# Second graph layer: the edge pass reads its source rows through a table of tiles in memory, and two loads become one

## The chip, the cores and the metric

One Trainium2 chip (trn2), one core. The metric is the device time of one execution in microseconds. The kernel before took 4205.64 us, the median of three runs (4204.25 to 4207.73).

## What is computed

3125 nodes with 64 features and 100000 edges sorted by their destination. Two attention layers (8 heads, then 4), a layer norm, then neighbour sums with three dense layers and a second norm. One attention layer, cut to what matters:

```
xl = (x @ Wl).reshape(N, heads, Dh);  xr = (x @ Wr).reshape(N, heads, Dh)
e = leaky_relu(xl[src] + xr[dst], 0.2)
logits = einsum('ehd,hd->eh', e, att)
a = exp(logits - segment_max(logits, dst)[dst])
alpha = a / segment_sum(a, dst)[dst]
out = segment_sum(alpha[:, :, None] * xl[src], dst)      # then the mean over heads, + bias
```

## The kernel before, in words

The sorted edges are cut into 800 tiles of 125 edges (T = 125, G = 800), the nodes into 98 windows of 32 (WN, NW). A unit is a pair of a tile and a window in which the tile has edges. Units are numbered so that unit = tile + window: 897 of them, padded to 900. A tile that spans two windows is in two units, and each of its units handles only the edges of its own window. The edge pass (`edge_pass`, lines 749 to 1236) goes through 45 chunks of 20 units (CU = 20).

Each unit needs two inputs in on-chip memory. `xs` holds the 125 source rows (64 floats each, 256 bytes). GpSimd (POOL) gathers them with one indirect DMA for a unit (line 820 in the pass, line 530 ahead of it); six chunks of buffers rotate (XR = 6), so POOL waits at line 817 until the sums of chunk c - 6 are done. `xw` holds the rows of the unit's window, split into three bf16 parts, 96 rows of 128 bytes. SyncE (SP) reads the window's number into a register (line 542, with a check of its bounds) and issues one DMA from `x3_d` at that address (line 543); three buffers rotate.

TensorE (PE) turns the 20 units of a chunk in five groups of four (`turn`, lines 873 to 889). Ahead of the first group it waits for all 20 gathers and all 20 window loads. Then come the projection (line 897), the logits (906, 909), the scans for the maxima on VectorE (DVE), the weights, and some three chunks later the weighted sums (948). SP also issues, in program order for every chunk: the list of window numbers of the next chunk (536), the destination numbers `dlb` (858), four loads of `lim` and four of `pre` for the chunk before (839, 841), and a store of maxima (865). PE's order is written out by hand; SP may be up to two chunks ahead of it (line 850).

In the second layer the node rows are computed just before. Two blocks precede the edge pass: `prepare_layer` (POOL gathers the first 35 units, EARLY) and `count_tables` (POOL gathers 45 more, up to 80 = `ahead` * 20). All engines meet at the end of each block. SP loads the windows of chunk 0 in `prepare_layer` (line 617) and those of chunk 1 only once the edge pass has begun. After the last chunk POOL gathers node maxima (826). `neighbour_sums` begins with a block that splits the rows in three parts (1604 to 1616).

Of the kernel before, what the change touches and what calls it, by code (L numbers as in the profile page):

```python
# [8 lines left out]
I32 = mybir.dt.int32  # L9
# [52 lines left out]
AHEAD = (1, 4)  # L62
EARLY = 35
# [10 lines left out]
class Layer:  # L74


    def __init__(self, nm, H, Wl, Wr, att, bias, x_node, x_rows, next_table, next_node, v_d, max_d, norm):
        self.nm, self.H, self.Wl, self.Wr, self.att, self.bias = nm, H, Wl, Wr, att, bias
        self.x_node, self.x_rows, self.next_table, self.next_node = x_node, x_rows, next_table, next_node
        self.v_d, self.max_d, self.norm, self.ahead = v_d, max_d, norm, AHEAD[1 if norm else 0]  # L80
# [125 lines left out]
def build_staircase(nc, k, a, ctx0, x0):  # L206
# [4 lines left out]
    k.src_idx = sbuf(nc, ctx0, "src_idx", [T, UT], I32)  # L211
    k.win_idx = sbuf(nc, ctx0, "win_idx", [BLK, NB], I32)
# [6 lines left out]
    with ExitStack() as ctx:  # L219
# [50 lines left out]
        no_key = sbuf(nc, ctx, "no_key", [1, 1])  # L270
        ps = [psum(nc, ctx, f"ps_setup{i}") for i in range(4)]
        s = {n: k.setup.enter_context(nc.semaphore("st_" + n)) for n in (
            "load", "iota", "ident0", "ident", "dve", "dve2", "dve3", "store", "transposed", "pad",
            "load2", "sides", "last", "upto2", "node", "keys", "lim", "x_pad", "dloc", "dl0", "row0", "pre", "pre_dma", "below0", "below")}
# [5 lines left out]
        with nc.Block() as block:  # L280
            @block.sync
            def _(sp):
                sp.dma_start(dg[:], a["dst"].rearrange("(p k e) -> p k e", k=KT, e=T)).then_inc(s["load"], 16)
                ld = Dma(sp, s["load2"])
# [17 lines left out]
                xs.wait()  # L302

# [78 lines left out]
        with nc.Block() as block:  # L382
            @block.vector
            def _(dve):
# [37 lines left out]
                link(dve.tensor_copy(k.dst_local[:, 5 * BLK:UT], ps[3][0:T, 0:4 * BLK]))  # L422
                dve.wait_ge(s["keys"], 16 * (2 * NB + 1))
# [37 lines left out]
            def _(act):  # L461
                for t in range(NT):
# [8 lines left out]
            def _(pe):  # L471
                pe.wait_ge(s["dve3"], NB + 2)
                for b in range(NB):
# [4 lines left out]
                                 k.ident[0:BLK, 0:BLK]).then_inc(s["transposed"], 1)  # L478

# [67 lines left out]
def prepare_layer(nc, k, ctx, lay):  # L547
# [24 lines left out]
    lay.node_of = sbuf(nc, ctx, lay.nm + "node_of", [128, HV * 128])  # L572
    with ExitStack() as tmp:
# [27 lines left out]
        with nc.Block() as block:  # L601
            @block.sync
            def _(sp):
# [12 lines left out]
                sp.wait_ge(lay.ld_w[0], 16)  # L616
                load_windows(k, sp, lay, fixed(0))
# [3 lines left out]
            def _(pool):  # L621
# [10 lines left out]
                fetch_rows(k, pool, lay, 0, EARLY if lay.norm else lay.ahead * CU)  # L632
# [116 lines left out]
def edge_pass(nc, k, lay):  # L749
# [12 lines left out]
    with ExitStack() as ctx:  # L762
# [5 lines left out]
        lim = [sbuf(nc, ctx, f"{nm}lim{r}", [128, SL + 1]) for r in range(3)]  # L768
        pre = [sbuf(nc, ctx, f"{nm}pre{r}", [128, SL]) for r in range(3)]
# [42 lines left out]
        with nc.Block() as block:  # L812
            @block.gpsimd
            def _(pool):
                for c in map(fixed, range(lay.ahead, NCH)):
# [14 lines left out]
            def _(sp):  # L830
                sp.wait_ge(s["init"], 8)

                def limits(c):
# [38 lines left out]
            def _(pe):  # L872
# [81 lines left out]
                pe.wait_ge(s["init"], 8)  # L954
# [25 lines left out]
            def _(act):  # L980
# [52 lines left out]
                act.wait_ge(s["init"], 8)  # L1033
# [29 lines left out]
            def _(dve):  # L1063
# [31 lines left out]
                def forward(c):  # L1095

                    r = c.slot(3)
                    dve.wait_ge(ld_l[r], c.uses(3) * 128)
# [944 lines left out]
```

## Time and profile before

| | |
|---|---|
| median of 3 runs | 4205.64 us |
| the profiled execution | 4214.95 us, of which the span is 4213.1 us |
| first layer's edge pass | 188 to 1854 us |
| second layer's `prepare_layer`, `count_tables` | 1963 to 2019 us, 2022 to 2098 us |
| second layer's edge pass | 2102 to 3580 us |
| neighbour sums and dense layers | 3670 us to the end |
| busy over the span: PE, DVE, ACT, POOL, SP's share of DMA packets | 80%, 69%, 40%, 69%, 11.3% of 16 DMA engines |

Times in rows are microseconds from the start of the span, durations of single instructions in nanoseconds where a row says min/median/max. "PEclk" is the granted share of TensorE's clock. Rows of the queue engines (SPq) are issuing work: the time for which SP is occupied with an instruction, not the transfer. In brackets stands the idle time before an instruction and what ended it.

### The profile page before, as it was taken

The numbers are of one execution on the slowest core, as the hardware profiler recorded it, in microseconds if no ns is written. First come the engines' busy times: TensorE is split into PE (matmuls) and PEld (weight loads), VectorE is DVE, ScalarE is ACT, GpSimd is POOL, SyncE is SP. The second block draws the span as 40 slices with busy tenths as digits, with TensorE's granted clock in tenths as the row PEclk, the third lists the DMA queues.
The fourth block names the chain that finished last, engine by engine and source line by source line (L and its number), as shares of the span: only waits on it lengthen the run. The fifth ranks groups of instructions, "written<-read, shape, count | busy, mean of one in ns | idle before, by whom it ended". The sixth has DMA issues, their size and how long they took to land. (4 is left out here: it accounts for less than half of the span.)

```text
span 4213.1 us, 81047 instructions
## 1 busy us (share of the span) xinstructions
PE 3388.3 (80%) x24299; PEld 2227.2 (53%) x24299; DVE 2892.4 (69%) x7435; ACT 1684.6 (40%) x3682; POOL 2891.8 (69%) x2226
## 2 busy tenths in 40 slices
PE   0499999999999999965178877777877776588896
PEld 0246666666666666654135545545554554355553
DVE  3568888888888888855426655555555555499982
ACT  3354444444444444413033333333333331256651
POOL 4488888887777777163747888888888883377750
PEclk9999999999999999957579988888888887599997
DMA  2234343343333333231123333333333331112110
GB/s 57 49 61 93 86 87 87 86 86 86 84 85 84 83 84 85 56 82 50 27 50 70 76 72 69 73 67 67 72 68 67 67 67 36 40 35 44 35 41 27
DMA packets 614978, 278.31 MB, mean 66 GB/s; under 512 B 452841, under 2 KB 575117, under 8 KB 613956
## 3 DMA queue, kind: packets, MB, share of 16 engines
q1 hardware_dynamic: 266160, 103.07, 11.3%
q0 software_dynamic: 110784, 80.17, 10.8%
q10 hardware_dynamic: 237600, 89.88, 8.7%
q8 instruction: 199, 3.26, 0.3%
q14 instruction: 235, 1.93, 0.2%
HBM read 164.01 MB, written 106.40 MB: 64 GB/s over the span
## 5 line engine op out<-in xcount | busy, mean ns | idle before, releaser
L897 PE MATMUL L_e_ps_z<-L_e_xT,L_w_abs 128*128 128x500 f32 x2700 | 1504.3, 643 | 1.9 <-issue 1.5
L820 POOL DMA_INDIRECT L_e_xs<-in_x_dram,src_idx x880 | 1196.0, 1359 | 337.2 <-issue 261.3
L820 POOL DMA_INDIRECT L_e_xs<-x_d,src_idx x820 | 1077.5, 1314 | 311.3 <-issue 249.4
L948 PEld LDWEIGHTS L_e_ps_v<-L_e_xs,L_e_p 125*128 125x128 f32 x5400 | 858.7, 204 | 655.6 <-issue 589.6
L993 ACT ACTIVATE L_e_rl<-L_e_ps_z 128x500 f32<-128x500 f32 x1350 | 790.0, 587 | 818.6 <-PE L_e_ps_z L897 610.1
L948 PE MATMUL L_e_ps_v<-L_e_xs,L_e_p 125*128 125x65 f32 x5400 | 798.9, 275 | 30.1 <-DVE L_e_acc L1177 25.0
L1177 DVE SCALAR_TENSOR_TENSOR L_e_acc<-L_e_acc,L_e_row,L_e_ps_v 128x130 f32<-128x130 f32 (+1 forms) x1440 | 449.5, 312 | 416.7 <-PE L_e_ps_v L948 218.9
L884 PE MATMUL L_e_ps_x<-ident,L_e_xs 125*64 125x125 f32 x1800 | 290.7, 287 | 301.5 <-DMA L_e_xs<-x_d,src_idx 255.7
L986 ACT ACTIVATE L_e_xT<-L_e_ps_x 128x500 f32<-128x500 f32 x450 | 264.5, 588 | 606.7 <-PE L_e_ps_x L887 447.9
L897 PEld LDWEIGHTS L_e_ps_z<-L_e_xT,L_w_abs 128*128 128x128 f32 x2700 | 427.4, 198 | 80.0 <-issue 31.1
L1160 DVE TENSOR_TENSOR L_e_p<-L_e_ohc,L_e_ae 125x640 f32<-125x640 f32 x540 | 427.1, 819 | 0.0
L1650 POOL DMA_INDIRECT g_xs<-x_d,src_idx x240 | 290.7, 1211 | 163.8 <-issue 59.1
L884 PEld LDWEIGHTS L_e_ps_x<-ident,L_e_xs 125*64 125x64 f32 x1800 | 189.6, 120 | 347.1 <-DMA L_e_xs<-x_d,src_idx 265.2
L1182 DVE SCALAR_TENSOR_TENSOR L_e_acc<-L_e_acc,L_e_keep,L_e_ps_v 128x65 f32<-128x65 f32 x540 | 134.8, 277 | 315.2 <-PE L_e_ps_v L948 237.9
L1088 DVE SCALAR_TENSOR_TENSOR L_e_f<-L_e_rl,L_sign 128x500 f32<-128x500 f32 x450 | 326.3, 726 | 14.6 <-issue 9.0
L1088 DVE SCALAR_TENSOR_TENSOR L_e_f<-L_e_rl,L_sign,L_e_f 128x500 f32<-128x500 f32 x450 | 330.4, 734 | 4.4 <-ACT L_e_rl L993 0.8
L1788 DVE TENSOR_SCALAR g_ohr<-t_rows_n,t_both 125x125 bf16<-125x125 bf16 x960 | 306.8, 326 | 3.3 <-PE g_ps_c L1701 2.6
L1764 ACT ACTIVATE g_cnt<-g_ps_c 125x400 bf16<-125x400 f32 x480 | 240.0, 503 | 170.2 <-PE g_ps_c L1701 150.7
L1789 DVE TENSOR_SCALAR g_ohk<-t_keys_n,t_both 125x200 bf16<-125x200 bf16 x960 | 304.1, 318 | 0.0
L1000 ACT ACTIVATE L_e_lg<-L_e_ps_l 128x125 f32<-128x125 f32 x450 | 123.6, 275 | 335.3 <-PE L_e_ps_l L909 261.2
L1701 PE MATMUL g_ps_c<-g_ohk,g_ohr 125*125 125x200 bf16 x960 | 182.8, 274 | 62.6 <-DVE g_ohk L1789 45.3
L906 PE MATMUL L_e_ps_l<-L_e_xT,L_w_lin 128*32 128x125 f32 x3600 | 192.2, 286 | 32.3 <-DVE L_e_f L1088 32.0
(305 smaller groups left out, 3853.4 us busy)
## 6 DMA issues: line engine op xcount, KB each, us to landing
L_v_d<-L_e_acc ACTq DMA_DIRECT2D x225, 260.0 KB
L_e_dlb<-dloc_d SPq DMA_DIRECT2D x90, 468.8 KB
L_v_d<-L_e_acc ACTq DMA_DIRECT2D x225, 130.0 KB
L_e_xw<-x_d SPq DMA_DIRECT2D x1800, 12.0 KB
L_e_xs<-in_x_dram,src_idx POOLq DMA_INDIRECT x900
L_e_xs<-x_d,src_idx POOLq DMA_INDIRECT x900
g_xs<-x_d,src_idx POOLq DMA_INDIRECT x240
L_e_lim<-lim_d SPq DMA_DIRECT2D x180, 19.5 KB
```

What stands on the lines that cost most here:

```text
L820: pool.indirect_dma_start(xs[c.slot(XR)][:, n, 0:D], None, lay.x_rows, bass.IndirectOffsetOnAxis(k.src_idx[:, u:u + 1], 0)).then_inc(gath[ ...
L884: pe.transpose(ps[0:D, j * T:(j + 1) * T], xs[r][:, n, 0:D], k.ident[0:T, 0:T])
L897: pe.matmul(ps_z[(C * g + part) % ZR][:, 0:QT], lay.w_abs[:, part * 128:(part + 1) * 128], xT[q][:], start=True, stop=True).then_inc(s["z_ ...
L948: ins = pe.matmul(ps_v[u // 2 % 2][:, u % 2 * VX + v * XW:u % 2 * VX + (v + 1) * XW], p[st % 3][:, u % NQ, v, :, :].rearrange("e n h -> e ...
L986: act.activation(xT[q][:], ps_x[g % 2][:, 0:QT], ACT.Copy).then_inc(s["xT_ready"], 1)
L993: act.activation(rl[n % NE][:], ps_z[n % ZR][:, 0:QT], ACT.Relu, scale=1.0 - SLOPE).then_inc(s["relu_done"], 1)
L1088: dve.scalar_tensor_tensor(out=f[g % 3][:], in0=rl[(C * g + part) % NE][:], scalar=lay.sign[:, part:part + 1], in1=rl[(C * g) % NE][:] if ...
L1160: ins = dve.tensor_tensor(p[n % 3][:, :, v, :, :], ohc[c.slot(2)][:, us, :].unsqueeze(3).to_broadcast([T, NQ, WN, HL]), ae[c.slot(2)][:, u ...
L1177: ins = dve.scalar_tensor_tensor(out=to, in0=prev, scalar=row[c.slot(2)][:, u:u + 1], in1=ps_v[u // 2 % 2][:, u % 2 * VX:(u % 2 + 1) * VX] ...
L1650: pool.indirect_dma_start(xs[p][:, j, :], None, table, bass.IndirectOffsetOnAxis(k.src_idx[:, u:u + 1], 0)).then_inc(gath[p], 16)
L1788: dve.tensor_scalar(ohr[v % HR][:], rows_n[:], both[:, v, 0:1], None, ALU.is_equal)
L1789: dve.tensor_scalar(ohk[v % HR][:], keys_n[:], both[:, v, 1:2], None, ALU.is_equal).then_inc(s["hot"], 1)
```

## The change

It gives the second layer (`lay.norm`) another way for `xs`. POOL gathers each tile once, 800 gathers, into four buffers of ten tiles; SP stores every ten tiles into a table in memory, `tiles_d`; and for every unit SP computes tile = unit - window from the register it already has and issues one more DMA, which loads the tile's 125 rows into `xs`. The indices of the tiles (`k.src_tile`) are made once in the set-up. POOL's gathers ahead of the edge pass grow from 35 + 45 units to 50 + 50 tiles; SP stores the first eight groups of ten there. In the pass, group e + 1 is stored half a chunk before the first unit that may need it, and group e + 4 is gathered after group e is stored. In the edge pass of this layer the window loads move behind `dlb` and the limits of the chunk before. For both layers: `lim` and `pre` come with one DMA of two rows, four instead of eight in a chunk, and the run-time check of the window's bounds is gone. 15 comparisons that make `winhot8` move from `count_tables` to the first block of `neighbour_sums`. The set-up gets one load, eight transposes and two copies more.

```diff
-AHEAD = (1, 4)
-EARLY = 35
+AHEAD = (1, 5)
+EARLY = 50
+TH = CU // 2
+TR = 4
+STORED = 8
+THS = G // TH
...
+def fetch_tiles(k, pool, lay, t0, t1):
+    for t in range(t0, t1):
+        e = t // TH
+        if t % TH == 0 and e >= TR:
+            pool.wait_ge(lay.t_store[e % TR], 16 * (e // TR))
+        pool.indirect_dma_start(lay.tiles[e % TR][:, t % TH, :], None, lay.x_rows,
+                                bass.IndirectOffsetOnAxis(k.src_tile[:, t:t + 1], 0)).then_inc(lay.t_gath[e % TR], 16)
+
+def store_tiles(k, sp, lay, e):
+    sp.wait_ge(lay.t_gath[e % TR], 16 * TH * (e // TR + 1))
+    sp.dma_start(bass.AP(lay.tiles_d.tensor, e * TH * D, [[G * D, T], [1, TH * D]]),
+                 lay.tiles[e % TR][:].rearrange("p u d -> p (u d)")).then_inc(lay.t_store[e % TR], 16)
+
+def stored(sp, lay, e):
+    sp.wait_ge(lay.t_store[e % TR], 16 * (e // TR + 1))
...
 def load_windows(k, sp, lay, c):
     for n in range(CU):
-        window = sp.value_load(lay.wins[c.slot(2)][0:1, n:n + 1], min_val=0, max_val=NW - 1)
+        e = 2 * c.number + n // TH
+        if lay.norm and n % TH == 0:
+            if (c.number == 0 or e + 1 >= STORED) and e + 1 < THS:
+                store_tiles(k, sp, lay, e + 1)
+            if e < THS:
+                stored(sp, lay, e)
+        u = min(c.val(CU, n), G + NW - 2)
+        window = k.nc.values_load(lay.wins[c.slot(2)][0:1, n:n + 1], engines=[mybir.EngineType.SP], min_val=max(0, u - G + 1), max_val=min(u, NW - 1),
+                                  skip_runtime_bounds_check_because="win_idx is the least of a count's rest and NW - 1")
+        if lay.norm:
+            sp.dma_start(lay.xs[c.slot(XR)][:, n, 0:D], bass.AP(lay.tiles_d.tensor, (u - window) * D,
+                                                                [[G * D, T], [1, D]])).then_inc(lay.gath[c.slot(XR)], 16)
         sp.dma_start(lay.xw[c.slot(3)][:, n, :], bass.AP(k.x3_d.tensor, window * (WN * S3),
                                                          [[D, 3 * WN], [1, D]])).then_inc(lay.ld_x[c.slot(3)], 16)
...
@@ prepare_layer
                 sp.wait_ge(lay.ld_w[0], 16)
+                if lay.norm:
+                    store_tiles(k, sp, lay, 0)
+                    sp.wait_ge(s["ones"], XR)
                 load_windows(k, sp, lay, fixed(0))
...
-                fetch_rows(k, pool, lay, 0, EARLY if lay.norm else lay.ahead * CU)
+                if lay.norm:
+                    fetch_tiles(k, pool, lay, 0, EARLY)
+                else:
+                    fetch_rows(k, pool, lay, 0, lay.ahead * CU)
@@ edge_pass
+                if lay.norm:
+                    fetch_tiles(k, pool, lay, lay.ahead * CU, G)
+                for c in map(fixed, range(lay.ahead, 0 if lay.norm else NCH)):
...
-                        sp.dma_start(lim[r][32 * j:32 * j + H, 0:SL],
-                                     bass.AP(k.lim_d.tensor, at, [[0, H], [1, SL]])).then_inc(ld_l[r], 16)
-                        sp.dma_start(pre[r][32 * j:32 * j + H, :],
-                                     bass.AP(k.pre_d.tensor, at, [[0, H], [1, SL]])).then_inc(ld_l[r], 16)
+                        sp.dma_start(both[r][32 * j:32 * j + H, :, 0:SL],
+                                     bass.AP(k.lim_d.tensor, at, [[0, H], [SLOTS, 2], [1, SL]])).then_inc(ld_l[r], 16)
...
-                        if c.after(1):
+                        if c.after(1) and not lay.norm:
                             sp.wait_ge(ld_w[c.slot(2)], c.uses(2) * 16)
                             load_windows(k, sp, lay, c)
...
                         limits(b)
+                    if lay.norm and c.there() and c.after(1):
+                        sp.wait_ge(ld_w[c.slot(2)], c.uses(2) * 16)
+                        if c.after(XR):
+                            sp.wait_ge(s["v_ready"], c.val(CU, CU * (1 - XR)))
+                        load_windows(k, sp, lay, c)
@@ count_tables
-                fetch_rows(k, pool, lay, EARLY, lay.ahead * CU)
+                fetch_tiles(k, pool, lay, EARLY, lay.ahead * CU)
...
+                for e in range(3, STORED):
+                    store_tiles(k, sp, lay, e)
...
-                for b in range(EB):
-                    link(dve.tensor_scalar(winhot8[:, b, :, :].rearrange("u j w -> u (j w)"), wins_n[0:BU, :], unit[:, b:b + 1], None, ALU.is_equal))
@@ neighbour_sums, first block
                     dve.tensor_tensor(rest[:], x_node[:], x3[:, :, 0, :], ALU.subtract).then_inc(s["rest"], 1)
+                    for b in range(EB):
+                        dve.tensor_scalar(winhot8[:, b, :, :].rearrange("u j w -> u (j w)"), wins_n[0:BU, :], unit[:, b:b + 1], None, ALU.is_equal)
                     dve.wait_ge(s["part"], 2)
```

## Rows read from the trace of the kernel before

**Rows 1.** Stretches, second edge pass: PE, PEld, DVE, ACT, POOL; PEclk, DMA, GB/s

```profile
2150.00:2290.00 140.00, 116.57 (x894) 70.96 (x894) 80.90 (x186) 55.24 (x126) 66.99 (x50) 0.90 0.29 57
2400.00:3400.00 1000.00, 775.91 (x5979) 506.98 (x5978) 582.94 (x1402) 349.56 (x810) 810.69 (x622) 0.87 0.36 69
```

**Rows 2.** Waits of PE, second edge pass: us, times, longest

```profile
PE L_e_ps_x L884 <- DMA L_e_xs<-x_d,src_idx: 255.7, 36, 8.6
```

**Rows 3.** Timeline of POOL, second pass: start, us, work, [idle before]

```profile
2223.39 1.22 POOL L820 DMA_INDIRECT L_e_xs<-x_d,src_idx  x1 [58.38 <-PE L_e_ps_v L948]
...
3485.99 1.21 POOL L820 DMA_INDIRECT L_e_xs<-x_d,src_idx  x1 [0.30 <-issue]
3540.92 1.24 POOL L826 DMA_INDIRECT L_node_max<-L_max_d,max_idx  x1 [53.72 <-DMA L_max_d<-L_e_me]
```

**Rows 4.** Lines 542 and 543 on SP, second pass: ns min/median/max

```profile
L542 SPq TENSOR_LOAD <-L_e_wins x845: 3/268/842, 2149.7 to 3435.9; - x169
L542 SPq FUSED_REGOPS  x845: 3/152/355, 2150.1 to 3436.5; - x169
L542 SPq SEQ_ASSERT  x845: 3/18/368, 2150.3 to 3436.7; - x169
...
L543 SPq FUSED_REGOPS  x845: 3/42/402, 2150.3 to 3436.7; - x169
L543 SPq MOVE L_e_xw<-x_d x845: 1/29/623, 2150.4 to 3436.8; - x169
L543 SPq DMA_DIRECT2D L_e_xw<-x_d x845: 3/322/1159, 2150.8 to 3436.9; - x169
```

**Rows 5.** Timeline of SP, two chunks of the second pass

```profile
2159.91 21.02 SPq L543 DMA_DIRECT2D L_e_xw<-x_d  x20
2180.98 0.33 SPq L536 DMA_DIRECT2D L_e_wins<-win_d  x1
2181.36 0.32 SPq L858 DMA_DIRECT2D L_e_dlb<-dloc_d  x1
2181.72 0.33 SPq L839 DMA_DIRECT2D L_e_lim<-lim_d  x1
...
2185.73 20.93 SPq L543 DMA_DIRECT2D L_e_xw<-x_d  x20
...
2806.27 22.41 SPq L543 DMA_DIRECT2D L_e_xw<-x_d  x20
2835.24 22.34 SPq L543 DMA_DIRECT2D L_e_xw<-x_d  x20
```

**Rows 6.** Timeline of POOL ahead of the pass, SP at its start

```profile
2017.88 1.21 POOL L530 DMA_INDIRECT L_e_xs<-x_d,src_idx  x1 [0.30 <-issue]
...
2024.81 1.23 POOL L530 DMA_INDIRECT L_e_xs<-x_d,src_idx  x1 [0.20 <-issue]
...
2097.22 1.21 POOL L530 DMA_INDIRECT L_e_xs<-x_d,src_idx  x1 [0.30 <-issue]
...
2107.44 21.52 SPq L543 DMA_DIRECT2D L_e_xw<-x_d  x20
```

**Rows 7.** Timeline of DVE: moved comparisons, and their new place

```profile
2087.12 8.44 DVE L1567 TENSOR_SCALAR t_winhot<-t_wins_n,t_unit 64x392 f32<-64x392 f32 x15
...
3678.58 1.83 DVE L1616 TENSOR_TENSOR g_x<-g_rest,g_x 125x1600 bf16<-125x1600 f32 x1 [1.60 <-ACT g_x L1609]
```

**Rows 8.** Timeline of PE, first layer, as its pass fills

```profile
223.31 0.65 PE L906 MATMUL L_e_ps_l<-L_e_xT,L_w_lin 128*32 128x125 f32 x8 [8.45 <-DVE L_e_f L1088]
```

**Rows 9.** SP's 1171.9 KB store, next issue; stores of 125 rows; ACT's packets

```profile
1970.89 0.29 SPq L147 DMA_DIRECT2D x_d<-L_x  x1
1984.09 21.75 SPq L543 DMA_DIRECT2D L_e_xw<-x_d  x20
...
L865 SPq DMA_DIRECT2D L_max_d<-L_e_me x32: 284/293/313, 2401.1 to 3378.9; - x32
...
q10 hardware_dynamic: 237600, 89.88, 8.7%
```

More of the change, by code:

```diff
@@ L270, in build_staircase @@
         no_key = sbuf(nc, ctx, "no_key", [1, 1])
+        sg = sbuf(nc, ctx, "sg", [BLK, KT, T], I32)
+        sgf = sbuf(nc, ctx, "sgf", [BLK, KT, T])
+        ps_s = [psum(nc, ctx, f"ps_tiles{i}") for i in range(2)]
         ps = [psum(nc, ctx, f"ps_setup{i}") for i in range(4)]
@@ L273, in build_staircase @@
             "load", "iota", "ident0", "ident", "dve", "dve2", "dve3", "store", "transposed", "pad",
-            "load2", "sides", "last", "upto2", "node", "keys", "lim", "x_pad", "dloc", "dl0", "row0", "pre", "pre_dma", "below0", "below")}
+            "load2", "sides", "last", "upto2", "node", "keys", "lim", "x_pad", "dloc", "dl0", "row0", "pre", "pre_dma", "below0", "below",
+            "load3", "src_f", "src_t")}
         k.setup_sems = dict(s)
@@ L302, in _ @@
                 xs.wait()
+                sp.wait_ge(s["load3"], 16)
             @block.gpsimd
@@ L422, in _ @@
                 link(dve.tensor_copy(k.dst_local[:, 5 * BLK:UT], ps[3][0:T, 0:4 * BLK]))
+                dve.wait_ge(s["src_t"], 1)
+                for h in range(2):
+                    link(dve.tensor_copy(k.src_tile[:].rearrange("p (b i) -> p i b", i=KT)[:, 4 * h:4 * h + 4, :],
+                                         ps_s[h][0:T, 0:4 * BLK].rearrange("p (i b) -> p i b", i=4)))
                 dve.wait_ge(s["keys"], 16 * (2 * NB + 1))
@@ L461, in _ @@
             def _(act):
+                act.activation(sgf[:], sg[:], ACT.Copy).then_inc(s["src_f"], 1)
                 for t in range(NT):
@@ L478, in _ @@
                                  k.ident[0:BLK, 0:BLK]).then_inc(s["transposed"], 1)
+                pe.wait_ge(s["src_f"], 1)
+                for b in range(KT):
+                    ins = pe.transpose(ps_s[b // 4][0:T, b % 4 * BLK:(b % 4 + 1) * BLK], sgf[:, b, :], k.ident[0:BLK, 0:BLK])
+                ins.then_inc(s["src_t"], 1)
             @block.sync
@@ L572, in prepare_layer @@
     lay.node_of = sbuf(nc, ctx, lay.nm + "node_of", [128, HV * 128])
+    if lay.norm:
+        lay.tiles = [sbuf(nc, ctx, f"{lay.nm}e_tiles{r}", [T, TH, D]) for r in range(TR)]
+        lay.t_gath = [semaphore(nc, k, f"{lay.nm}e_t_gath{r}") for r in range(TR)]
+        lay.t_store = [semaphore(nc, k, f"{lay.nm}e_t_store{r}") for r in range(TR)]
     with ExitStack() as tmp:
@@ L767, in edge_pass @@
         row = [sbuf(nc, ctx, f"{nm}row{r}", [128, CU + 1]) for r in range(2)]
-        lim = [sbuf(nc, ctx, f"{nm}lim{r}", [128, SL + 1]) for r in range(3)]
-        pre = [sbuf(nc, ctx, f"{nm}pre{r}", [128, SL]) for r in range(3)]
+        both = [sbuf(nc, ctx, f"{nm}lim{r}", [128, 2, SL + 1]) for r in range(3)]
+        lim = [both[r][:, 0, :] for r in range(3)]
+        pre = [both[r][:, 1, 0:SL] for r in range(3)]
         xT = [sbuf(nc, ctx, f"{nm}xT{r}", [128, QT]) for r in range(5)]
@@ L814, in _ @@
             def _(pool):
-                for c in map(fixed, range(lay.ahead, NCH)):
+                if lay.norm:
+                    fetch_tiles(k, pool, lay, lay.ahead * CU, G)
+                for c in map(fixed, range(lay.ahead, 0 if lay.norm else NCH)):
                     if c.after(XR):
@@ L1189, in _ @@
                 for r in range(3):
-                    dve.memset(lim[r][:], -BIG).then_inc(s["init"], 1)
-                    dve.memset(pre[r][:], -BIG).then_inc(s["init"], 1)
-                dve.wait_ge(s["init"], 8)
+                    dve.memset(both[r][:], -BIG).then_inc(s["init"], 1)
+                dve.wait_ge(s["init"], 5)
                 spread_hot(fixed(0))
@@ L1439, in __init__ @@
         self.winhot = sbuf(nc, ctx, nm + "winhot", [BLK, PB, NW])
-        self.winhot8 = sbuf(nc, ctx, nm + "winhot8", [BU, EB, Q, NW])
+        self.wins_n = sbuf(nc, ctx, nm + "wins_n", [BLK, Q * NW])
+        self.unit = sbuf(nc, ctx, nm + "unit", [BU, EB])
         self.both = sbuf(nc, ctx, nm + "both", [T, EU, 2])
@@ L1448, in count_tables @@
     nm = "t_"
-    winhot, winhot8, both, rows_n, keys_n = tab.winhot, tab.winhot8, tab.both, tab.rows_n, tab.keys_n
+    winhot, both, rows_n, keys_n, wins_n, unit = tab.winhot, tab.both, tab.rows_n, tab.keys_n, tab.wins_n, tab.unit
     s = {n: semaphore(nc, k, nm + n) for n in ("iota", "load", "before", "dve", "split", "picked")}
@@ L1479, in count_tables @@
         ok = sbuf(nc, ctx, nm + "ok", [T, EU])
-        wins_n = sbuf(nc, ctx, nm + "wins_n", [BLK, Q * NW])
         win_f = sbuf(nc, ctx, nm + "win_f", [BLK, NB])
-        unit = sbuf(nc, ctx, nm + "unit", [BU, EB])
         HALF = EU // 2
@@ L1593, in neighbour_sums @@
     AT = [0, 0, 0, 5, 9, 13, 17, 21, NT]
-    winhot, winhot8, both, rows_n, keys_n = tab.winhot, tab.winhot8, tab.both, tab.rows_n, tab.keys_n
+    winhot, both, rows_n, keys_n, wins_n, unit = tab.winhot, tab.both, tab.rows_n, tab.keys_n, tab.wins_n, tab.unit
     with ExitStack() as octx:
         nm = "g_"
+        winhot8 = sbuf(nc, octx, nm + "winhot8", [BU, EB, Q, NW])
         x3 = sbuf(nc, octx, nm + "x3", [T, NT, 3, D], BF16)
```

33 lines of the change are left out of this document (18 added, 15 removed).

## The prediction, made before the changed kernel ran

> **What bounds the kernel now.** I read the stretches of the second edge pass first. Once the pass is full TensorE is busy 776 us in 1000, GpSimd 811; in the earlier stretch TensorE is busy 117 in 140, at a somewhat higher granted clock (0.90 against 0.87) [rows 1]. So TensorE is not the limit of the later stretch. The waits of PE say what is: 255.7 us in 36 waits, all ahead of the first turn of a chunk, for the gathered rows `xs` [rows 2], 7 us in nearly every chunk. Then GpSimd's timeline: after 120 units it waited 58 us for a free buffer, began again at 2223.4, and its last gather ended at 3487.2 [rows 3]. Nothing held it between the two: (3487.2 - 2223.4) / 780 = 1.62 us a gather, 32.4 us a chunk of 20. That is the pace of the pass. From the last gather to the first gather of node maxima (3540.9 [rows 3]) the pipeline drains, 54 us that the change leaves alone.
>
> SyncE must be read too, since the change gives it work. For each unit it runs six instructions with medians of 268, 152, 18, 42, 29 and 322 ns [rows 4], in all 0.83 us. 20 of them take 20.93 us from the first DMA to the end of the last [rows 5]: (20.93 - 0.32) / 19 = 1.085 us a unit, so 0.042 us lie between two instructions. The next chunk's loads start 2185.73 - 2159.91 = 25.8 us later [rows 5], and in that stretch SyncE has no wait to speak of. In the full pass the same 20 take 22.4 us, 7% more [rows 5], and it idles until TensorE frees a buffer. SyncE is thus busy for 26 to 27 of 32.4 us before anything is added.
>
> **The change, part by part.**
>
> *Gathers.* 800 tiles in place of 900 units. But 20 tiles a chunk are still asked for until tile 800, in chunk 39; the saving is all at the end, where five chunks need no gather.
>
> *Ahead of the pass.* GpSimd gathers 100 in place of 80. In the first block the last of 35 ended at 2019.1; 15 more at 1.21 + 0.30 = 1.51 us take 23 us. In the second, 45 took from 2024.8 to 2098.4, 1.64 us each; 5 more take 8 us [rows 6]. In both blocks GpSimd is the last to finish (VectorE's last work before was done at 2095.6 [rows 7]), so the pass begins 31 us later. The seven stores that SyncE adds there, and the 20 loads of chunk 0, lie beside these gathers. In the old kernel the later start would be made good by having more in hand. SyncE has nothing in hand: it loads chunk 1 only in the pass, at 2107.4 before [rows 6] and at 2138.6 now.
>
> *SyncE, one unit.* Out: the bounds check, 0.152 + 0.018 and two gaps, 0.254 us. In: register arithmetic for (unit - window) x 64, a MOVE, a DMA. The multiplication for `xw` takes 0.042 and the check's several comparisons 0.152; these are the bounds, and I take two simple operations, 0.08 (a gain down to nothing is possible if it is folded into its neighbour). MOVE: 0.029. A store of 125 rows takes SyncE 0.293 and a load at a register's address 0.322 [rows 4, 9]; I take 0.308. With three gaps, 0.543. A unit: 1.085 - 0.254 + 0.543 = 1.374, bounds 1.32 and 1.46. Under load the old unit took 0% to 7% more [rows 5]; I take 2%, so 1.40, and 28.0 for a chunk.
>
> *SyncE, the rest of a chunk.* 25.8 - 21.7 = 4.1 in the chunk of rows 5, and 0.34 for the store of maxima that joins later. Four DMAs of limits fewer at 0.34 give back 1.36. Two stores of ten tiles cost 0.34 each and their waits some 0.1. In all 3.9. **The new period is 31.9 us** (bounds: 30.3, and 31.2 + 3.9 = 35.1). SyncE is then the slowest, slower than TensorE, whose work is 0.776 x 32.4 = 25 us [rows 1], and just under GpSimd's old 32.4 us.
>
> *The end of the pass.* The loads of chunk 44 are issued by 2138.6 + 43 x 31.9 + 28.1 = 3538.4, less 3.4 for five chunks without stores: 3535, against 3487.2 for the last gather. So +48 us. Although each chunk is slightly quicker, SyncE pays 44 of them from 2138.6, where GpSimd paid 39 from 2223.4; the lead gathered beforehand is lost.
>
> *GpSimd in the pass.* Tiles from 120 on need a buffer whose store (the ninth) SyncE issues in the middle of chunk 3: 2138.6 + 63.8 + 14, and some 4 for landing, 2220. Then 680 gathers at 1.62: 3322. SyncE wants the last group at the start of chunk 39, 2138.6 + 38 x 31.9 = 3351. GpSimd is 29 us early: hidden, but no more than that.
>
> *Moved and small parts.* `winhot8`: 8.44 us leave VectorE where GpSimd hid them, and go to a block where VectorE had 1.60 us to spare [rows 7]: +7. First layer: TensorE is its bound, so SyncE's lighter work is hidden, except while the pass fills, where a wait of 8.45 us follows from SyncE's first chunk [rows 8]; 20 x 0.254 us sooner: -5, nothing at worst. The set-up loads 390.6 KB more ahead of `x`; at the rate of rows 9 (1171.9 KB in at most 13.2 us) at most 4 us, at least nothing: +2. Its copies and transposes lie beside a wait for loads. Three larger memsets replace six of the same bytes: nothing, or 1 us if that is not so.
>
> Sum: 48 + 7 - 5 + 2 = **+52 us**. The profiled execution took 4214.95 us, 9.3 above the median of the runs; 4214.95 + 52 - 9.3 = 4258.
>
> **A rule of the skill, weighed.** What the transfers do to the DMA engines: the store of 1171.9 KB was over within 13.2 us, 91 GB/s [rows 9], while in the full pass the engines are 36% busy [rows 1]. The trace of before does not say on how many engines a transfer of 125 rows runs. The Trainium skill ("DMA: Bandwidth & Descriptors", on why a DMA increments its semaphore by 16) says that the generator takes the largest number up to 16 that divides the outer dimensions of both sides, and the lowest-numbered engines: for 125 rows always the same five. By that the new loads and stores would pile up there; it speaks against this change, and is the third rival.
>
> **The rivals.**
>
> *1. SyncE is cheap: faster.* For it: the register work may fold, and 20.93 us show chunks without any stall [rows 5]. With 1.32 us a unit the period is 30.3; the last load is issued at 2138.6 + 43 x 30.3 + 26.4 - 3.4 = 3464.5, if gathers also drop to 1.21 + 0.30 = 1.51 us [rows 3]. -23 + 4 = -19: 4187. With register work free it would be some 4130. Against: every unit needs a second DMA of 0.3 us, and gathers ran at 1.62.
>
> *2. GpSimd still sets the pace.* If SyncE is under about 31.1 us but gathers stay at 1.62, the last group is there at 3322, and chunk 39's loads and five chunks follow: 3322 + 2 + 26.4 + 5 x 29.6 = 3498. +11 + 4 = +15: 4221. So a fast SyncE alone wins nothing. With gathers of 1.59 it is no change.
>
> *3. Five DMA engines fill up: much slower.* A chunk then asks of each of the five: two stores of 312.5 KB at 91 GB/s, 7 us; 500 packets of 256 bytes, at the mean of ACT's packets, 0.087 x 16 x 4213 / 237600 = 24.7 ns [rows 9], 12.4 us; and the old 36% of 32.4 us, 11.7 us. That is 31.1, just under the period. At 33 ns a packet it is 35.2; 43 x (35.2 - 31.9) = +142 more: 4400. Against: the packets counted in rows 9 are larger (378 bytes on average), so ours should be cheaper.
>
> *4. The check of bounds stays in the program.* 20 x 0.254 x 1.02 = 5.2 us a chunk, +224: 4480.
>
> The case on the other side is the first; it decides if the period falls under about 30.7 us and the gathers under 1.58 us together.
>
> **The numbers.** Forecast (SyncE paces, period 31.1 to 33.5; 4224 to 4327 by 43 us for each us of period): 0.50. Rival 1: 0.22. Rival 2: 0.15. Rival 3: 0.10. Rival 4: 0.03. The likeliest gives 4258. The range leaves out rivals 3 and 4 and the lower part of rival 1: 4180 to 4345. Faster by over 0.2% (8 us, about what a measurement of this kernel can tell from no change): rival 1 but for its edge, 0.20. Within 0.2%: that edge, most of rival 2's quick side and the forecast's lowest, 0.13. Slower: 0.67.
>
> **What would show it.** Right: SyncE's issue without a wait from 2138 to some 3535; two DMAs a unit, 27.5 to 28.5 us for 20 units; TensorE waits 5 to 7 us at each chunk for loads of `xs` or `xw` issued by SyncE, not for gathers; GpSimd waits for stores in the pass. The first gather of maxima is near 3588 (3540.9 before), the pass starts 31 us later, VectorE's first block of neighbour sums is 7 us longer. Wrong: a unit of SyncE under 1.32 or over 1.46 us; waits of SyncE on gathers (rival 2) or on its own stores' landing with a high DMA share (rival 3); a pass that starts before 2125.

## The result, and the profile after

The changed kernel takes 4524.99 us (median of 4 runs, 4520.24 to 4543.79) and the kernel before 4204.94 (4 runs, 4200.35 to 4207.73): a ratio of 1.0772, 95% interval 1.0753 to 1.0791. It is 7.7% slower. The direction was forecast (0.67), the size was not: 4258 was forecast, and the range ended at 4345. The profiled execution took 4526.7 us, 2 above the median.

First the two stretches of [rows 1] in the changed kernel: PE, PEld, DVE, ACT, POOL busy, the granted clock, the DMA share, and GB/s.

```profile
2150.00:2290.00 140.00, 80.64 (x618) 45.91 (x617) 47.11 (x101) 41.67 (x93) 50.60 (x40) 0.78 0.30 65
2400.00:3400.00 1000.00, 636.33 (x4972) 418.97 (x4964) 483.25 (x1167) 296.96 (x674) 675.74 (x517) 0.81 0.42 90
```

In the full pass TensorE is busy 636 us in 1000 in place of 776, and GpSimd 676 in place of 811. Neither is the bound. The granted clock, a mean over stretches at 1.2 and at 2.4 GHz, fell from 0.87 to 0.81 while TensorE idled more. The DMA engines move 90 GB/s in place of 69 and are still under half busy. The waits of PE and of POOL in the pass say for whom they wait:

```profile
PE L_e_ps_x L953 <- DMA L_e_xs<-tiles_d: 565.4, 42, 16.7
PE L_e_ps_v L1017 <- DVE L_e_acc L1246: 5.5, 7, 1.8
```

```profile
POOL L_node_max L892 <- DMA L_max_d<-L_e_me: 310.1, 1, 310.1
POOL L_e_tiles L561 <- DMA tiles_d<-L_e_tiles: 306.6, 63, 65.5
```

After 2200 us TensorE waits 565 us in 42 waits for rows loaded from the table, against 256 us in 36 for gathered rows in the whole pass before [rows 2]. GpSimd waits 307 us for stores of tiles, and is done long before the end: it then waits 310 us for the node maxima (54 before [rows 3]). Both wait for work that SyncE issues; SyncE itself shows no wait in the pass.

SyncE's timeline (start, time occupied by the issue): the first units of chunk 1; the two lists around chunk 2, in which no tile is stored; a store of ten tiles and what follows; two lists with two stores between them; the last load.

```profile
2137.13 0.33 SPq L594 DMA_DIRECT2D L_e_xs<-tiles_d  x1
2137.64 0.35 SPq L596 DMA_DIRECT2D L_e_xw<-x_d  x1
2138.74 0.30 SPq L594 DMA_DIRECT2D L_e_xs<-tiles_d  x1
2140.30 0.29 SPq L594 DMA_DIRECT2D L_e_xs<-tiles_d  x1
...
2168.06 0.28 SPq L578 DMA_DIRECT2D L_e_wins<-win_d  x1
2201.96 0.27 SPq L578 DMA_DIRECT2D L_e_wins<-win_d  x1
...
3147.91 0.32 SPq L568 DMA_DIRECT2D tiles_d<-L_e_tiles  x1
3149.26 0.29 SPq L594 DMA_DIRECT2D L_e_xs<-tiles_d  x1
3149.74 2.03 SPq L596 DMA_DIRECT2D L_e_xw<-x_d  x1
3152.79 0.29 SPq L594 DMA_DIRECT2D L_e_xs<-tiles_d  x1
...
3166.74 0.29 SPq L578 DMA_DIRECT2D L_e_wins<-win_d  x1
3204.96 0.29 SPq L578 DMA_DIRECT2D L_e_wins<-win_d  x1
...
3802.01 0.32 SPq L596 DMA_DIRECT2D L_e_xw<-x_d  x1
```

Chunk 1 begins at 2137.1 (2138.6 was forecast). A unit takes 2140.30 - 2138.74 = 1.56 us, not 1.40. From list to list a chunk without stores takes 33.9 us and the one at 3166 takes 38.2; the mean of 32 chunks in the middle of the pass is 38.9. Behind a store the next loads are held: 3149.26 to 3152.79 is 3.5 us for one unit. The last load is issued at 3802, 267 us later than forecast (3535).

The instructions of the unit. Each row gives the operation, minimum, median and maximum in ns, and the first and last start; first those of the pass, then the register load of the first layer, where one DMA per unit precedes it:

```profile
L591 SPq TENSOR_LOAD <-L_e_wins x876: 429/462/2337, 2136.4 to 3797.6; - x176
L594 SPq DMA_DIRECT2D L_e_xs<-tiles_d x900: 292/293/1542, 1996.6 to 3801.6; - x180
L594 SPq FUSED_REGOPS  x895: 57/57/85, 1999.5 to 3798.5; - x179
L596 SPq FUSED_REGOPS  x1790: 37/37/51, 156.5 to 3799.0; - x199
...
L591 SPq TENSOR_LOAD <-L_e_wins x895: 260/269/803, 156.0 to 1677.9; - x179
```

The added DMA and register work cost no more than was forecast (0.293 for 0.308, and 0.057 for 0.08). What was not in the sum is the first row: the same register load, 0.268 us in the kernel before [rows 4] and 0.269 in this kernel's first layer, takes 0.462 in the pass.

GpSimd's timeline: its wait at tile 120, its last gather, and its first gather of node maxima (3485.99 and 3540.92 in [rows 3]).

```profile
2226.09 1.22 POOL L561 DMA_INDIRECT L_e_tiles<-x_d,src_tile  x1 [65.55 <-DMA tiles_d<-L_e_tiles]
...
3543.88 1.41 POOL L561 DMA_INDIRECT L_e_tiles<-x_d,src_tile  x1 [0.30 <-issue]
3855.44 1.61 POOL L892 DMA_INDIRECT L_node_max<-L_max_d,max_idx  x1 [310.14 <-DMA L_max_d<-L_e_me]
```

The maxima come 314.5 us later than before, and the whole span is 4524.6 - 4213.1 = 311.5 longer. The first layer's maxima start at 1814.54 (1814.41 before), so up to there the two kernels are level. The loads of chunk 1 begin 30 us later (2137.1 for 2107.4 [rows 6]), because more is gathered ahead, as forecast; the rest of the loss is in the pass.

### The profile page after: what moved, and what is told of

Its sections match the earlier page's. It is cut to its first block and busy times, and to the rows that moved or that the text cites. A ratio compares the mean times of both kernels' runs of the same rounds, so it can differ in the third digit from the quotient of the medians.

```text
span 4524.6 us, 80645 instructions
## 1 busy us (share of the span) xinstructions
PE 3378.8 (75%) x24307; PEld 2226.4 (49%) x24307; DVE 2884.0 (64%) x7431; ACT 1705.8 (38%) x3683; POOL 2739.5 (61%) x2126
## 5 line engine op out<-in xcount | busy, mean ns | idle before, releaser
L886 POOL DMA_INDIRECT L_e_xs<-in_x_dram,src_idx x880 | 1180.4, 1341 | 349.0 <-issue 261.0
L561 POOL DMA_INDIRECT L_e_tiles<-x_d,src_tile x800 | 1041.8, 1302 | 535.0 <-DMA tiles_d<-L_e_tiles 306.6
L892 POOL DMA_INDIRECT L_node_max<-L_max_d,max_idx x50 | 62.8, 1256 | 438.1 <-DMA L_max_d<-L_e_me 423.5
L1779 PE MATMUL g_ps_s<-g_x,g_cnt 125*128 125x192 bf16 x1500 | 185.7, 249 | 28.0 <-DVE g_sums L1863 14.0
## 6 DMA issues: line engine op xcount, KB each, us to landing
L_e_xs<-tiles_d SPq DMA_DIRECT2D x900, 31.2 KB
tiles_d<-L_e_tiles SPq DMA_DIRECT2D x80, 312.5 KB
```

The lines of the kernel that those rows point to most:

```text
L561: pool.indirect_dma_start(lay.tiles[e % TR][:, t % TH, :], None, lay.x_rows, bass.IndirectOffsetOnAxis(k.src_tile[:, t:t + 1], 0)).then_in ...
L886: pool.indirect_dma_start(xs[c.slot(XR)][:, n, 0:D], None, lay.x_rows, bass.IndirectOffsetOnAxis(k.src_idx[:, u:u + 1], 0)).then_inc(gath[ ...
```

## The experiments

Parts undone or added alone come first (e1 to e4, beside them the kernel before at 4208.71), then combinations. A time is that of one run where no interval is given, and a time in brackets stands for the difference from the changed kernel; the loss under study is 320 us. "Period" is the time from list to list on SyncE, for a chunk without stores and as the mean over 32 chunks in the middle.

**e1, the bounds check put back** (rival 4's price).

```diff
-        window = k.nc.values_load(..., min_val=..., max_val=..., skip_runtime_bounds_check_because="...")
+        window = k.nc.values_load(..., min_val=..., max_val=...)
```

> The changed kernel with the run-time check of the window's bounds put back. My pricing in the prediction took 0.254 us a unit for the check: then 20 x 0.254 = 5.1 us more in each of 44 chunks, 4525 + 224 = about 4750 us. Rival theory: the changed kernel's register load takes 0.462 us where the old one took 0.268 and was followed by 0.152 of comparisons, so the comparisons only waited for the load's value, and the check was nearly free: then the load falls back to about 0.27, the comparisons show 0.15, and a unit grows by at most 0.1 us, 4525 + 0 to 90 = 4525 to 4615 us.

4730.84, against 4524.99 for the changed kernel. It costs 206 us, some 0.23 us for each of 900 units; the first units go from 1.56 to 1.81 (2142.06 - 2140.25, 2143.87 - 2142.06):

```profile
2140.25 0.30 SPq L593 DMA_DIRECT2D L_e_xs<-tiles_d  x1
2142.06 0.29 SPq L593 DMA_DIRECT2D L_e_xs<-tiles_d  x1
2143.87 0.29 SPq L593 DMA_DIRECT2D L_e_xs<-tiles_d  x1
```

The price of the check, 0.254, stands, and the idea that the check was hidden behind a slow register load falls: the load keeps its 0.46 us and the check comes on top. (The check stands behind the load in a unit, so the load follows its two DMAs as closely as before; this run says nothing on what the load waits for.)

**e2 and e3, transfers of 128 rows.** Tile buffers and table get three rows more (zeros). e3 changes the stores alone, e2 the loads of `xs` too.

```diff
-    sp.dma_start(bass.AP(lay.tiles_d.tensor, e * TH * D, [[G * D, T], [1, TH * D]]),
+    sp.dma_start(bass.AP(lay.tiles_d.tensor, e * TH * D, [[G * D, 128], [1, TH * D]]),
...
-                                                                [[G * D, T], [1, D]])).then_inc(lay.gath[c.slot(XR)], 16)
+                                                                [[G * D, 128], [1, D]])).then_inc(lay.gath[c.slot(XR)], 16)
```

> The changed kernel with 128 rows in place of 125 in the tile buffers, the table and xs (three rows of zeros are carried along, the results do not use them), so stores of tiles and loads of xs have an outer dimension of 128. Theory A: the 2 to 3 us for which SyncE stands still after each store of tiles come from the few DMA engines that a transfer of 125 rows uses; on more engines the stalls fall under 1 us, some 3 to 4 us a chunk over 37 chunks, 110 to 150 us in all: 4375 to 4415 us. Theory B: the stall belongs to the store as such, or SyncE's instruction stream alone counts: 4505 to 4545 us.

> As the run with 128 rows everywhere, but the loads of xs stay at 125 rows; only the stores of tiles have 128. If the stores alone make the stalls, the same time as with 128 rows everywhere, within 15 us. If the 20 loads of xs in a chunk fill the few engines, most of the time stays: over 4480 us.

e3: 4436.54 (-88), between its two forecasts. e2: 4376.10 (-149), inside the forecast of its theory A, but in part by luck: theory A had the whole gain in the stalls behind stores. Stores of 128 rows bring the period with stores from 38.9 to 35.9, against 34.3 without them: two stores cost 1.6 us of a period in place of 5.0 (38.9 against 33.9; either figure holds 0.35 for the store of maxima that falls in the same chunks). The other 60 us are the loads, and not by a shorter stall: a chunk without stores falls from 34.3 to 32.1. The register load in the pass shows it, first e3, then e2:

```profile
L591 SPq TENSOR_LOAD <-L_e_wins x876: 97/462/899, 2146.2 to 3699.5; - x176
```

```profile
L591 SPq TENSOR_LOAD <-L_e_wins x876: 3/269/696, 2146.6 to 3634.1; - x176
```

With `xs` loads of 128 rows it is back at 0.269 us. The issue of the `xs` load went up (median 342 ns against 293), so a unit gained less than 0.19.

How many shares a transfer has can be counted in the same traces, from the times at which it raises its semaphore. In the changed kernel each of the 72 stores of the pass raises it six times: once 0.47 us after the issue, then five times, the first at 5.1 us and the last at 6.6 us (medians). A store of 128 rows raises it 16 times, from 2.3 to 4.2 us (e5, where nearly all are recorded).

**e4, ten window numbers to one register load.**

```diff
-        window = k.nc.values_load(lay.wins[c.slot(2)][0:1, n:n + 1], ...)
+        if n % 10 == 0:
+            _, windows = k.nc.values_load_multi_w_load_instructions(
+                lay.wins[c.slot(2)][0:1, n:n + 10], engines=[mybir.EngineType.SP], min_val=0, max_val=NW - 1, ...)
+        window = k.nc.s_assert_within(windows[n % 10], ...)
```

> The changed kernel, but SyncE reads ten window numbers into ten registers with one instruction in place of one for each unit (values_load of [1, 10]). If SyncE's own instructions set the pace of the second edge pass, as its unbroken issue in the trace says, a unit falls by some 0.4 us (0.462 + 0.042 out, a tenth of a longer load in), 8 us a chunk, from 38.3 to about 30: then GpSimd's gathers become the limit near 32 to 33 us and the time is 4200 to 4290 us. If the landing of transfers sets the pace, SyncE issues faster and waits more, and the time stays above 4450 us.

4301.80, -223, 12 above its forecast: SyncE's instructions are the pace. A chunk without stores takes 26.4 to 27.4 us. With stores it takes 33.9: the register load issued right behind a store is held. The 88 loads of the pass take 4 us at the median:

```profile
L592 SPq TENSOR_LOAD <-L_e_wins x88: 1125/3966/6789, 2140.1 to 3559.6; - x88
```

**e5 and e6, both together, then stores sooner.** e6 issues each store about when its gathers should be done, by a fixed table.

```diff
-            if (c.number == 0 or e + 1 >= STORED) and e + 1 < THS:
-                store_tiles(k, sp, lay, e + 1)
+            for t in STORE_AT.get(e, ()):
+                store_tiles(k, sp, lay, t)
...
+for t in range(STORED, THS):
+    STORE_AT.setdefault(min(t - 1, 2 + max(0, -(-(t - 9) * 5 // 4))), []).append(t)
```

> Ten window numbers to a register load, and 128 rows in stores and loads of tiles (three rows more than there is data for, zeros). Theory S: what held SyncE in the changed kernel was the register loads and the transfers of 125 rows that run on few DMA engines. With both gone a chunk with stores takes SyncE 27 to 28 us in place of 37; then GpSimd's gathers set the pace again: the 680 of the pass begin near 2215 and take 1.62 us each, so the last ends near 3320, and the rest of a chunk and five chunks without gathers follow: the last load near 3475, time 4190 to 4225. Theory R: a batched register load is held by any store issued just ahead of it, whatever its rows; the period stays at 32 to 33 us as in the run with the batch alone, and the time at 4285 to 4305.

> The same, and each store of ten tiles is issued about when its gathers are done instead of half a chunk ahead of its load. If GpSimd's wait for free buffers at tile 120 (47 us) is what is left of the loss, its gathers now run through from 2134 to about 3270, the last load is near 3420, and the time 4130 to 4170: under the kernel before. If gathers, loads or TensorE are slowed by something else in the pass, no more than 15 us are gained on the run above.

e5: 4258.68, between the two forecasts. Loads of 128 rows are slower to issue (a unit of 1.11 us against 1.02 with 125), and a chunk without stores takes 28.9. e6: 4255.73, a miss. GpSimd no longer stood 50 us at tile 120, but it waited 52 us in eight waits between 2339 and 2594, where the table of stores was later than the gathers; its last gather was at 3323.9 (3322.3 in e5). What the miss shows is that GpSimd's waits were not on the path: SyncE waits for no gather in either run, its middle period is 32.0 us in e5 and 31.8 in e6, and it is still the bound.

**e7, the register load ahead of the store** (e4, 125 rows, one block moved up).

> Batch of ten, 125 rows, as in the earlier run (4301.8), but the register load is issued ahead of the store of tiles, not behind it. There the load behind a store took 4 to 6 us. If the store holds only the register load behind it, 2 to 3 us are saved at each of 72 stores: 4180 to 4240, with register loads of about 2.2 us. If the stall moves to the DMA instructions behind the store (five engines take 125 rows, and their queues are full), the time stays at 4280 to 4310.

4226.88, -75 on e4 and inside the first forecast, with register loads at 1.77 us:

```profile
L587 SPq TENSOR_LOAD <-L_e_wins x88: 1102/1774/2752, 2140.2 to 3488.5; - x88
```

**e8 and e15, other numbers of rows.** e8: 120 rows in stores and loads; e15: 112 rows in the loads alone. The rest of each tile's rows is left out.

```diff
-            sp.dma_start(lay.xs[c.slot(XR)][:, n, 0:D], bass.AP(..., [[G * D, T], [1, D]]))...
+            sp.dma_start(lay.xs[c.slot(XR)][0:112, n, 0:D], bass.AP(..., [[G * D, 112], [1, D]]))...
```

> The changed kernel with stores and loads of 120 rows in place of 125: the last five edges of each tile are left out (memory is filled once, so they are constants), and with them parts of the result. If it is the number of DMA engines that counts (120 rows divide into 15 or 8 parts, 125 into 5), it does what 128 rows did: register loads near 0.27 us in place of 0.46, a period near 32.7 us, 4365 to 4395. If 128 helped because all partitions or 16 engines take part in equal shares, it stays near 4525.

> The changed kernel with loads of 112 rows of a tile in place of 125 (13 edges of each tile are left out and memory is filled once, so parts of the result are other numbers); the stores keep 125 rows. If a register load is quick when the transfers ahead of it are shared out over all 16 DMA engines (112 is 16 times 7; 125 goes to 5 engines and 120 to 15), it takes 0.27 us in place of 0.46 and the time falls by 50 to 90 us, to 4435 to 4475. If only a full 128 rows helps, the load stays at 0.46 us and the time within 20 us of 4525.

e8: 4551.21, 26 over the changed kernel: 15 parts instead of 5 gain nothing in total. e15: 4452.69, as the theory of all 16 engines has it. The kernel before took 4235.27 beside e15, and e15's chunk 1 began 27 us later than the changed kernel's, so its periods say more than the total: 30.9 and 31.2 us without stores (33.9), 36.4 in the middle (38.9). The register load in the pass, e8 and then e15:

```profile
L591 SPq TENSOR_LOAD <-L_e_wins x864: 430/462/1564, 2146.2 to 3798.5; - x173
```

```profile
L591 SPq TENSOR_LOAD <-L_e_wins x876: 3/270/1695, 2163.1 to 3715.2; - x176
```

0.46 us behind 125 and 120 rows, 0.27 behind 112 and 128. In e8 the issue of an `xs` load went up to 360 ns, which is why a unit took 1.62 us; its pair of stores cost 3.0 us of a period (38.8 against 35.8), between the 5.0 of 125 rows and the 1.6 of 128. The Trainium skill ("DMA: Bandwidth & Descriptors") has a transfer shared out over the largest number of engines up to 16 that divides its rows: 5, 15, 16 and 16 for 125, 120, 112 and 128. The semaphores agree with it: five late increments for a store of 125 rows, fifteen of 120 (2.4 to 4.3 us), sixteen of 128. So do the stalls behind stores, in their order. The register load does not follow the number of shares: it is the same with 5 and 15, and short with 16. What 125 and 120 rows have in common here is the one early increment (0.47 and 0.58 us behind the issue of a store), which 128 rows lack. Whether the long register load hangs on it is not shown.

**e9 and e10, e7 with early stores; then 80 tiles ahead in place of 100.**

```diff
-AHEAD = (1, 5)
-EARLY = 50
+AHEAD = (1, 4)
+EARLY = 35
```

> The run with the register load ahead of the store (4226.9), and the stores of tiles issued about when their gathers are done. There GpSimd stood 50 us at tile 120 and then gathered without a pause from 2214 to 3310, and SyncE's chunks took 31 us beside it against 26 without stores. If GpSimd's late start is what is left, its gathers end near 3270, the last load is near 3425 to 3450 (3510 there), and the time 4140 to 4170. If SyncE itself needs some 31 us for a chunk with stores, because DMA instructions behind a store are held, the last load stays near 3500 and the time within 15 us of 4227.

> The same with 80 tiles gathered ahead of the pass, 35 of them in the first block, as the kernel before has it, in place of 100 and 50. The pass starts 31 us sooner. If SyncE is the bound, it gains that: 20 to 31 us on the run before this one. If GpSimd's gathers are, nothing is gained, or up to 15 us are lost because the lead is smaller.

e9: 4230.00, as slow as e7 and as its second forecast has it: one of the instructions just behind a store is held (the longest of them takes 1.0 us at the median, and 1.1 in e7). GpSimd waited 48 us in six waits between 2332 and 2565, and SyncE for no gather. e10: 4212.00, -18, just under its first forecast. The pass starts 23 us sooner, not 31 (its first gather at 2108.9 for 2132.0).

**e12 and e13, the stores issued by ScalarE,** with the register loads as they are, and batched.

```diff
+                    if lay.norm and c.there() and q % 2 == 0 and q:
+                        e = 2 * c.number + 5 + q // 2
+                        if STORED <= e < THS:
+                            store_tiles(k, act, lay, e)
```

> The changed kernel, with the 72 tile stores of the pass issued by ScalarE, one chunk earlier, and all else as it is. SyncE's chunks without stores take 32.6 us, those with stores 37.1. If a store holds the queue of the engine that issues it, SyncE's chunks all take 33 us and the time is 4340 to 4375. If the five DMA engines that a store of 125 rows uses are held for everybody, SyncE's loads of 125 rows wait as before: over 4480.

> The same with ten window numbers to a register load. If the queue theory holds, SyncE needs 26 to 27 us a chunk and GpSimd's gathers pace the pass at 32.4 us; they run on from near 2190 because stores come earlier, end near 3285, and the time is 4170 to 4215. If the DMA engines themselves are held, it stays at 4225 to 4300.

e12: 4502.07, -23 only, as its second forecast has it. SyncE's middle period is 38.0 without a single store in its own queue (38.9 with two). So what a store of 125 rows holds isn't the queue that issues it; the other queue's loads are held as well. Here too single register loads reach 2.5 us, though no store stands ahead of them in SyncE's queue:

```profile
L591 SPq TENSOR_LOAD <-L_e_wins x876: 440/462/2522, 2138.7 to 3767.9; - x176
```

e13: 4205.67, inside what the queue theory forecast, which e12 has just refuted. Its time was met by luck. The theory wanted 26 to 27 us a chunk; SyncE took 31.1 in the middle and 27.1 to 28.1 where no stores run, without a wait for gathers, so the stores of the other queue cost it some 4 us a chunk here as well.

**e11 and e14, the kernel before with batched register loads and no check,** nothing else; e14 is e11 in five runs.

```diff
-        window = sp.value_load(lay.wins[c.slot(2)][0:1, n:n + 1], min_val=0, max_val=NW - 1)
+        if n % 10 == 0:
+            _, windows = k.nc.values_load_multi_w_load_instructions(lay.wins[c.slot(2)][0:1, n:n + 10], ...)
+        window = windows[n % 10]
```

> The kernel before with ten window numbers to a register load and no bounds check, nothing else. SyncE was not its bound, so the time stays within 10 us of the kernel before, though SyncE's unit falls from 1.085 to some 0.6 us. If it is over 15 us faster, the gains of the batch in the other runs are no sign of what the table costs.

> The kernel before with batched register loads and no bounds check, timed against the kernel before. The one look gave 4174.6 against 4204.9, because SyncE's first chunks of the second pass took 17 us in place of 25 and GpSimd's wait at tile 120 fell from 58 to 22 us. If that is the mechanism, the gain is 25 to 35 us, 0.6% to 0.8%. If it was chance, under 8 us.

e11: 4174.64 beside 4204.94: the forecast that nothing would happen is missed, by SyncE's chunks of 17.5 us at the start of the pass, for 25.8. e14: 4171.89 (5 runs) against 4206.65, ratio 0.9919, interval 0.9905 to 0.9934. GpSimd's wait at tile 120:

```profile
2190.74 1.71 POOL L824 DMA_INDIRECT L_e_xs<-x_d,src_idx  x1 [23.22 <-PE L_e_ps_v L952]
...
3446.03 1.21 POOL L824 DMA_INDIRECT L_e_xs<-x_d,src_idx  x1 [0.30 <-issue]
3501.24 1.34 POOL L830 DMA_INDIRECT L_node_max<-L_max_d,max_idx  x1 [54.01 <-DMA L_max_d<-L_e_me]
```

It ends at 2190.7, not 2223.4 [rows 3]; the last gather comes 40 us sooner and the maxima too. In the kernel before, SyncE's first chunks of 25.8 us [rows 5] held VectorE, which waits for `dlb` behind the window loads, and VectorE held TensorE, which held the buffers. VectorE's waits for `dlb` until GpSimd goes on, in the kernel before and in e14, and TensorE's waits in the kernel before, which come at the pace of SyncE's chunks:

```profile
DVE L_e_oht L1068 <- DMA L_e_dlb<-dloc_d: 62.8, 5, 23.5
...
DVE L_e_oht L1072 <- DMA L_e_dlb<-dloc_d: 33.4, 5, 15.8
...
2161.25 0.65 PE L906 MATMUL L_e_ps_l<-L_e_xT,L_w_lin 128*32 128x125 f32 x8 [5.73 <-DVE L_e_f L1088]
2187.05 0.64 PE L906 MATMUL L_e_ps_l<-L_e_xT,L_w_lin 128*32 128x125 f32 x8 [5.44 <-DVE L_e_f L1088]
```

The batch and the check were taken out together, so their shares in the 34 us are not told apart.

**e16 and e17, the table without its price:** e10 with stores of 128 rows and loads of 125; e17 is e16 in five runs.

> Batch of ten ahead of the stores, stores as soon as gathered, 80 tiles ahead (4212.0), and the stores with 128 rows. There two stores made SyncE's chunk about 4 us longer (26 to 30), as in the changed kernel (32.6 to 37.1), where 128 rows cut it to 1.1. If so here, SyncE's chunks with stores fall to 27 or 28 us, the gathers pace the pass, and the time is 4150 to 4190. If the stall is of another kind with batched loads, it stays at 4200 to 4220.

> The kernel of the run with 128-row stores, batched register loads ahead of them and 80 tiles ahead, timed. If the table with its price removed is worth something, it is faster than the kernel before by 0.3% or more (under 4193 where that takes 4206). If the one look was flattered by a slow run of the kernel before beside it, the two are within 0.3% of each other, 4193 to 4219. Either way it should be slower than the kernel before with batched register loads (4171.9).

e16: 4200.08, 10 above its forecast, beside 4235.27 for the kernel before. e17: 4160.06 (5 runs, 4151.46 to 4166.94) against 4201.19, ratio 0.9897, interval 0.9881 to 0.9913. It gains 1.0% on the kernel before, as the first forecast has it. It was expected to stay behind e14 (0.9919) and did not; the two intervals overlap, so which of the two is faster is not shown. GpSimd's gathers of tiles, and the windows of [rows 1]:

```profile
L564 POOL DMA_INDIRECT L_e_tiles<-x_d,src_tile x800: 1205/1209/2568, 1967.5 to 3269.4; - x160
...
  issue: 243.3, 798
```

```profile
2400.00:3400.00 1000.00, 803.21 (x6231) 528.45 (x6231) 605.99 (x1456) 373.00 (x845) 706.84 (x538) 0.88 0.47 107
```

798 of its 800 gathers follow the one before by their issue alone, with no wait for a store. SyncE's chunks with stores take 27.3 to 29.4 us until 2591; from there it keeps to the gathers' pace, 32.3. Now it is SyncE that waits for gathers, 85 us in 38 waits:

```profile
SPq L571 <- DMA L_e_tiles<-x_d,src_tile: 85.0, 38, 4.0
```

TensorE is busy 803 us in 1000 (776 before).

## Why the prediction was wrong, point by point

- *What bounds the kernel before.* Half right. GpSimd's 1.62 us a gather is the pace from 2223 on. What set 2223 was not asked; SyncE set it, and "a fast SyncE alone wins nothing" (rival 2) fell with e14, -34 us: there SyncE's work alone was made lighter.
- *Ahead of the pass.* Right: chunk 1 begins at 2137.1 for 2138.6. The set-up and the first layer came out at 0 (+2 and -5 were forecast).
- *SyncE, one unit: 1.40.* **The first step that failed.** The register load was carried over at 0.268, and it took 0.462; all the rest of the unit together came out 0.01 under the 1.374 of the sum. A unit is 1.555 at the median, 0.155 over the forecast (which had 2% for load in it): 20 x 0.155 x 43 = 133 us.
- *SyncE, the rest of a chunk: 3.9, with two stores at 0.34 and their waits 0.1.* **The second.** A pair of stores cost 5.0 us of the period in all, with the store of maxima, for 1.1 forecast; the rest is stalls of the instructions behind. The middle period is 38.9 for 31.9 forecast; less the 3.1 of the units, 3.9 x 36 = 140 us. 133 and 140 make 273, and the last load was 267 late. Neither stall was in the sum: it took single instructions at the medians of a kernel in which no such transfers stood ahead of them.
- *Rival 3, five DMA engines fill up, 0.10.* It looked in the right place, the rows of a transfer, with a working that was wrong. It asked whether the engines' time in a chunk suffices, which gave "just under the period", and its 33 ns a packet stands in no row; the DMA share is 0.42. What counts is how long the instructions behind one store are held, some 2 us each time, and that lands on SyncE because SyncE is the bound. Full engines explain only the second failed step at best: the long register load is the same with 15 shares as with 5 (e8). Even so the rule of the Trainium skill ("DMA: Bandwidth & Descriptors") that spoke against the change deserved more than a tenth.
- *GpSimd hidden.* Right: it waited 307 us for stores, since SyncE was slower still. A store took longer to land than the 4 us assumed: issued at 2220.1, it let GpSimd go on at 2226.1.
- *Drain.* Right: from the last load to the maxima 3855.4 - 3802.0 = 53.4 us, as 54 were left alone.
- *`winhot8`: +7.* Half: between the two subtractions lie 3997.61 - 3990.87 = 6.74 us in place of 3678.58 - 3675.15 = 3.43, so +3.3. The 15 comparisons took 5.08 us there, not 8.44. Before, then after:

```profile
3675.15 1.83 DVE L1614 TENSOR_TENSOR g_rest<-x,g_x 125x1600 f32<-125x1600 f32 x1 [11.46 <-ACT g_x L1607]
3678.58 1.83 DVE L1616 TENSOR_TENSOR g_x<-g_rest,g_x 125x1600 bf16<-125x1600 f32 x1 [1.60 <-ACT g_x L1609]
...
3990.87 1.83 DVE L1680 TENSOR_TENSOR g_rest<-x,g_x 125x1600 f32<-125x1600 f32 x1 [11.77 <-ACT g_x L1673]
3992.61 5.08 DVE L1682 TENSOR_SCALAR g_winhot<-t_wins_n,t_unit 64x392 f32<-64x392 f32 x15
3997.61 1.81 DVE L1684 TENSOR_TENSOR g_x<-g_rest,g_x 125x1600 bf16<-125x1600 f32 x1
```

Shown: SyncE is the bound (e1, e4); the rows of the stores make most of their stall (e3), and it isn't the issuing queue's (e12); the rows of the loads make the register load long (e2, e8, e15). The semaphores show the number of shares too, 5, 15 and 16. Argued only: that the stall is a wait for the few lowest-numbered DMA engines; no row names an engine. Left open: why a register load is long behind a load of 125 or 120 rows; and why the issue of an `xs` load costs 293, 317, 342 and 360 ns with 125, 112, 128 and 120 rows.

## What to carry to other kernels

Don't price the instructions of an engine that issues transfers by their old medians when other transfers will stand ahead of them: the same register load took 0.27 or 0.46 us here, and a load of ten numbers 2.8 to 6.8 us right behind a large store. Give a large store rows that divide by 16, zeros if need be (e3: -88 us). For small loads it depends: 128 rows paid with single register loads (e2), but with batched ones their slower issue made a unit 1.11 us for 1.02 (e5), and the fastest table kernel (e17) has loads of 125 rows. Load several registers at once, and do it ahead of a large store. And where one engine sets the pace, ask who set its start: the 58 us wait of GpSimd in the kernel before was mostly SyncE's (23 us are left in e14), and lighter register work (loads in tens, no check) was worth 0.8% even without the table.

## What was not expected of the hardware

- A register load takes 0.27 us behind one DMA of 96 rows, and behind two if the one from the table has 112 or 128 rows (e15, e2); 0.46 if it has 125 or 120 (the changed kernel, e8). Ten numbers in one load take 1.1 us at the least, 1.8 at the median (e7), and 2.8 to 6.8 right behind a store of 125 rows (e4, median 4.3).
- A store of 312.5 KB in 125 rows lengthens the loads of another engine's queue too (e12: period 38.0 without a store in SyncE's own queue, 34.5 at the end of the pass, where there are no stores).
- In 128 rows the same store costs a third of it, 1.6 us a pair for 5.0 (e3).
